# Self attentions of a four layer decoder: turns interleaved with value products, scores ahead of both, exponential ahead of the turned evictions

## What is computed

```
s = q @ k.T * scale            # 100 x 100, causal in layers 0, 1 and 3
p = softmax(s)                 # row maximum taken off, exponential, divided by the sum
y = p @ v                      # v has 8 columns a head, in layer 2 it has 16
x = x + (y @ Wo + b)           # layers 0, 1, 3
# layer 2, differential attention, two score matrices a head:
y = p1 @ v - lam * (p2 @ v);  y = y / sqrt(mean(y*y) + eps) * w;  x = x + y @ Wo
```

## Time and profile before

| | |
|---|---|
| median of three executions | 6178.4 us (6163.06 to 6204.71) |
| the profiled execution | 6208.25 us, span of the core 6206.5 us |
| PE busy | 4731.2 us, 76% of the span |
| DVE, ACT, POOL busy | 3437.1, 2441.8, 1999.7 us |
| mean granted TensorE clock | 0.818 |
| sa0, half batches (first turn to last value product) | 167.6 us |
| sa1 | 139.2 us |
| sa2 | 355.6 us |
| sa3 | 167.3 us |

### The profile page before, as it was taken

One profiled execution on the slowest core, in us unless ns is written; L12 is line 12 of the kernel. 1 busy time (PEld: TensorE's weight loads), 2 busy tenths in 40 slices (PEclk: granted clock), 3 DMA queues, 4 the chain that ended last, 5 costly groups with the idle time before them and its releaser, 6 DMA issues. The chain is left out here.

```text
span 6206.5 us, 84643 instructions
## 1 busy us (share of the span) xinstructions
PE 4731.2 (76%) x22582; PEld 3354.9 (54%) x22582; DVE 3437.1 (55%) x5067; ACT 2441.8 (39%) x3674; POOL 1999.7 (32%) x1091
## 2 busy tenths in 40 slices
PE   7999999999798866669878888888486444432698
PEld 6778778888544755348845555555274222221344
DVE  3444444444345422444556666664646999987444
ACT  2345555555222311123335555554123555540122
POOL 0055555555100000000036666664001555550000
PEclk7789999999799965687779999998677666655699
DMA  2100000000011312121111112110020000000011
GB/s 74 48 8 16 16 16 16 16 16 8 13 42 29 70 36 58 41 82 31 28 43 43 42 42 46 43 38 20 11 43 20 22 21 21 21 16 0 5 46 38
DMA packets 153375, 193.27 MB, mean 31 GB/s; under 512 B 91760, under 2 KB 136576, under 8 KB 152864
## 3 DMA queue, kind: packets, MB, share of 16 engines
q1 hardware_dynamic: 152992, 188.87, 12.5%
HBM read 134.07 MB, written 19.05 MB: 25 GB/s over the span
## 5 line engine op out<-in xcount | busy, mean ns | idle before, releaser
L1021 POOL TENSOR_TENSOR pexp_lo<-arena,pexp_hi 128x800 fp32r<-128x800 f32 x384 | 727.8, 1895 | 413.8 <-POOLq L1020 413.8
L976 POOL TENSOR_TENSOR pexp_lo<-arena,pexp_hi 128x800 fp32r<-128x800 f32 x384 | 628.4, 1636 | 515.6 <-POOLq L975 515.6
L1947 DVE TENSOR_REDUCE arena<-ps 128x1 f32<-128x482 f32 (+3 forms) x624 | 393.3, 657 | 404.1 <-DVEq L1925 388.9
L2092 DVE TENSOR_REDUCE arena<-ps 100x1 f32<-100x482 f32 (+1 forms) x768 | 476.6, 656 | 219.0 <-DVEq L2061 200.7
L1282 ACT ACTIVATE arena<-ps 128x800 f32<-128x800 f32 x384 | 322.3, 839 | 554.1 <-ACTq L1280 552.2
L1348 ACT ACTIVATE arena<-ps 128x800 f32<-128x800 f32 x384 | 321.7, 838 | 402.2 <-ACTq L1342 396.8
L2399 DVE MATCH_REPLACE8 arena<-arena 100x1444 f32<-100x1444 f32 x256 | 423.0, 1673 | 0.0
L3022 PE MATMUL ps<-kst,qs 96*100 96x482 f32 (+1 forms) x768 | 334.0, 436 | 116.4 <-PEq L2982 112.5
L1732 DVE TENSOR_REDUCE arena<-ps 100x8 f32<-100x800 f32 x160 | 158.7, 992 | 392.1 <-DVEq L1729 392.1
L3260 PE MATMUL ps<-arena,chunk 128*128 128x400 f32 x648 | 286.3, 524 | 72.6 <-PEq L3259 72.5
L2652 PE MATMUL ps<-w_const,arena 100*100 100x100 f32 x2560 | 311.2, 287 | 37.9 <-PEq L2648 37.9
(11 more groups left out here) (358 smaller groups left out, 11004.8 us busy)
## 6 DMA issues: line engine op xcount, KB each, us to landing
ctxT<-in_ctxT SPq DMA_DIRECT2D x64, 541.5 KB
ctxk<-in_ctx SPq DMA_DIRECT2D x48, 528.0 KB
kst<-mid SPq DMA_DIRECT2D x128, 180.5 KB, 3.1
heads_dram<-arena SPq DMA_DIRECT2D x20, 800.0 KB
chunk<-in_ff_chunks SPq DMA_DIRECT2D x77, 193.0 KB, 2.4
arena<-gate_dram SPq DMA_DIRECT2D x64, 200.0 KB, 3.1
kst<-xn SPq DMA_DIRECT2D x64, 180.5 KB, 2.9
q_rows<-heads_dram SPq DMA_DIRECT2D x36, 200.0 KB
```

What stands on the lines that cost most here:

```text
L976: own(nc.gpsimd.tensor_tensor(pexp_lo[p % 3][:, :, :], pexp[p % 3], pexp_hi[p % 3][:, :, :], ALU.subtract))
L1021: own(nc.gpsimd.tensor_tensor(pexp2_lo[p % 3][:, :, :], pexp2[p % 3], pexp2_hi[p % 3][:, :, :], ALU.subtract))
L1947: peak = nc.vector.tensor_reduce(mparts[0:at.stop - at.start, m, c:c + 1], bank(k, z - a, at.stop - at.start), AX.X, ALU.max)
L2092: peak = nc.vector.tensor_reduce(mparts2[:, h, c:c + 1], bank(k, z - a, S), AX.X, ALU.max)
```

## The change

PE: in each k it now waits for the exponential of k first; then come the four unread matmuls, into the score banks that scores(k + 2) will fill, then scores(k + 2), and then turns(k, k - 1): one turn of k, one value product of k - 1, and so on, eight times. The wait for o_free and v_ready (values_wait) stands ahead of the first turn, and the wait for an eviction of k - 1 ahead of each group of four. Sides follow as before. ACT: the exponential of k + 1 goes ahead of the sides and of the evictions of k. For sa2, the sums of squares (squared_sums) stay at k = 2 and the rest of finish moves to k = 3, features go to k = 4 and 5 and project to k = 6. No matmul, eviction or DMA is added or taken away.

```diff
--- before.py
+++ after.py
@@ -598,7 +598,8 @@
 
 
     VALUES_AT = {1: (0, 1, 2, 6), 2: (0, 1)}
-    TURNS_AT = {1: (3,), 2: (3, 4)}
+    TURNS_AT = {1: (3,), 2: (4, 5)}
+    PROJECT_AT = {1: 5, 2: 6}
 
     def all_units(nsm, unit):
 
@@ -1181,13 +1182,17 @@
                 if not first and k in TURNS_AT[nsm]:
                     features(k - TURNS_AT[nsm][0])
 
+            def exponential(k):
+                act.wait_ge(s.shifted, 1)
+                act.sem_inc(s.shifted, -1)
+                nc.scalar.activation(probs[:, k % 2, :].rearrange("p (c t) -> p c t", c=2),
+                                     ps[0:S, 2 * (k % 2):2 * (k % 2) + 2, 0:GT], ACT.Exp,
+                                     scale=float(cfg["scale"])).then_inc(s.probs_ready, 1)
+
             def unit(u, par, first=False, last=False):
                 for k in range(8):
-                    act.wait_ge(s.shifted, 1)
-                    act.sem_inc(s.shifted, -1)
-                    nc.scalar.activation(probs[:, k % 2, :].rearrange("p (c t) -> p c t", c=2),
-                                         ps[0:S, 2 * (k % 2):2 * (k % 2) + 2, 0:GT], ACT.Exp,
-                                         scale=float(cfg["scale"])).then_inc(s.probs_ready, 1)
+                    if k < 7 or not last:
+                        exponential((k + 1) % 8)
                     if not first and k == 2 and cfg.get("diff"):
                         root()
                     if k > 0:
@@ -1202,6 +1207,7 @@
 
             for i in range(4 // nsm):
                 value_rows(0, i, i)
+            exponential(0)
             all_units(nsm, unit)
             if cfg.get("diff"):
                 root()
@@ -1750,13 +1756,16 @@
                     dve.sem_inc(s.o_free, 1)
                     done(nc.vector.scalar_tensor_tensor(y, second, col[0:S, 6:7], y, ALU.mult, ALU.add))
 
-            def finish(par):
+            def squared_sums(par):
                 if cfg.get("diff"):
                     y = y_tok[:, par, :]
-                    y3 = y.rearrange("p (h w) -> p h w", w=16)
                     done(nc.vector.tensor_tensor(y_sq, y, y, ALU.mult))
                     done(nc.vector.tensor_reduce(y_rms[:, :], y_sq.rearrange("p (h w) -> p h w", w=16), AX.X, ALU.add))
                     dve.sem_inc(s.rms_sum, 1)
+
+            def finish(par):
+                if cfg.get("diff"):
+                    y3 = y_tok[:, par, :].rearrange("p (h w) -> p h w", w=16)
                     dve.wait_ge(s.rms_root, 1)
                     dve.sem_inc(s.rms_root, -1)
                     done(nc.vector.reciprocal(y_rms[:, :], y_rms[:, :]))
@@ -1786,6 +1795,8 @@
                     if not first and k in (0, 2):
                         normalise(k // 2 + 2, 1 - par)
                     if not first and k == 2:
+                        squared_sums(1 - par)
+                    if not first and k == nsm + 1:
                         finish(1 - par)
                     if not first and k == 7:
                         update(u - 1)
@@ -1795,6 +1806,7 @@
             all_units(nsm, unit)
             normalise(2, 1)
             normalise(3, 1)
+            squared_sums(1)
             finish(1)
             update(4 * nsm - 1)
             dve.wait_ge(s.q_stack_free, 1)
@@ -2634,41 +2646,40 @@
                     last = mm(bank(2 * (k % 2) + c, GT, S), q[:, sm, g, at], keys[:, sm, g, :, at], start=not cfg["causal"], stop=True)
                 last.then_inc(s.scores, 1)
 
-            def unread(n):
-
-                for i in range(n):
-                    mm(bank(4 + i % 2, GT, S), ident_bf[0:S, 0:S], causal_bf[:, :], start=True, stop=True)
-
-            def turn(k, first):
-                if not first:
-                    pe.wait_ge(s.probsT_ready, 2)
-                    pe.sem_inc(s.probsT_ready, -2)
-                unread(4)
-                pe.wait_ge(s.probs_ready, 1)
-                pe.sem_inc(s.probs_ready, -1)
-                for c in range(2):
-                    for j in range(4):
-                        at = c * GT + j * S
-                        last = mm(bank(4 + c, S, S, j * S), probs[:, k % 2, at:at + S], ident[0:S, 0:S], start=True, stop=True)
-                    last.then_inc(s.turned, 1)
-
-            def values(k, par):
+            def values_wait(k):
+
                 slot, half = k // 2, k % 2
-                i, sm = slot // nsm, slot % nsm
                 if half == 0:
                     pe.wait_ge(s.o_free, 1)
                     pe.sem_inc(s.o_free, -1)
-                if half == 0 and sm == 0:
+                if half == 0 and slot % nsm == 0:
                     pe.wait_ge(s.v_ready, 1)
                     pe.sem_inc(s.v_ready, -1)
+
+            def value(k, par, c, j):
+                slot, half = k // 2, k % 2
+                h = 8 * half + 4 * c + j
+                at = 16 * (vw + 1) * (slot // nsm) + h * (vw + 1)
+                ins = mm(bank(7, vw + 1, S, h * (vw + 1)), probsT[:, k % 2, c * GT + j * S:c * GT + j * S + S],
+                         vaug[:, par, at:at + vw + 1], start=True, stop=True)
+                if h == 15:
+                    ins.then_inc(s.o_full, 1)
+
+            def turns(k, behind, par):
+
+                if behind is not None:
+                    values_wait(behind)
                 for c in range(2):
+                    if behind is not None:
+                        pe.wait_ge(s.probsT_ready, 1)
+                        pe.sem_inc(s.probsT_ready, -1)
                     for j in range(4):
-                        h = 8 * half + 4 * c + j
-                        at = 16 * (vw + 1) * i + h * (vw + 1)
-                        last = mm(bank(7, vw + 1, S, h * (vw + 1)), probsT[:, k % 2, c * GT + j * S:c * GT + j * S + S],
-                                  vaug[:, par, at:at + vw + 1], start=True, stop=True)
-                if half == 1:
-                    last.then_inc(s.o_full, 1)
+                        at = c * GT + j * S
+                        ins = mm(bank(4 + c, S, S, j * S), probs[:, k % 2, at:at + S], ident[0:S, 0:S], start=True, stop=True)
+                        if j == 3:
+                            ins.then_inc(s.turned, 1)
+                        if behind is not None:
+                            value(behind, par, c, j)
 
             def features(par, c):
                 if c == 0:
@@ -2693,20 +2704,23 @@
 
             def unit(u, par, first=False, last=False):
                 for k in range(8):
-                    turn(k, first and k == 0)
+                    pe.wait_ge(s.probs_ready, 1)
+                    pe.sem_inc(s.probs_ready, -1)
+                    for i in range(4):
+                        mm(bank(2 * (k % 2) + i % 2, GT, S), ident_bf[0:S, 0:S], causal_bf[:, :], start=True, stop=True)
                     if k < 6:
                         scores(k + 2, par)
                     elif not last:
                         scores(k - 6, 1 - par)
                     if k > 0:
-                        values(k - 1, par)
-                    elif not first:
-                        values(7, 1 - par)
+                        turns(k, k - 1, par)
+                    else:
+                        turns(0, None if first else 7, 1 - par)
                     if k in VALUES_AT[nsm] and not last:
                         value_rows(u + 1, VALUES_AT[nsm].index(k))
                     if not first and k in TURNS_AT[nsm]:
                         features(1 - par, k - TURNS_AT[nsm][0])
-                    if not first and k == 5:
+                    if not first and k == PROJECT_AT[nsm]:
                         project()
 
             for i in range(per):
@@ -2716,7 +2730,10 @@
             all_units(nsm, unit)
             pe.wait_ge(s.probsT_ready, 2)
             pe.sem_inc(s.probsT_ready, -2)
-            values(7, 1)
+            values_wait(7)
+            for c in range(2):
+                for j in range(4):
+                    value(7, 1, c, j)
             for c in range(nsm):
                 features(1, c)
             project()
```

## The result

The changed kernel takes 6362.51 us (median of four executions, 6321.25 to 6405.49), the kernel before 6174.53 us on the same chip (6163.06 to 6204.71): a ratio (of the means) of 1.0297 with a 95% interval of 1.0207 to 1.0387. It is slower by 3%, 188 us. The forecast was 6300 us, slower, in a range of 6130 to 6410.

What follows compares the result with a forecast made beforehand. PE's work and its clock were taken to bound the kernel. sa2 +94, sa0 and sa3 +15 each, starts +5 made +129 us: 6337 profiled, 6307 against the median, said as 6300; range 6130 to 6410.

Steps and rivals of the forecast that it cites:

- The stall of sa2 is moved: sa2, k = 3: PE waits for o_free before its first turn, 4.9 us, against 4.3 before.
- every second unit: sa2, units 1 to 7: the clock rises in every second unit, so 59 us is taken between 55 and 63.
- the walk: sa2: a unit followed at full clock through PE, DVE and ACT; PE stands from 13.6 to 18.5 us at k = 3.
- The clock: sa2: runs free of value products shrink from 4.75 to 2.1 us, 3.6 with the projection; far fewer rises expected.
- the sum: Whole kernel: sa2 +94, sa0 and sa3 +15 each, sa1 0, starts +5; together +129 us.
- the unit: sa2, units 1 to 7: 59 us each, against some 45.6 before; 7 times 13.4 is +94 us.
- sa0 and sa3: Both stages: ten of 32 half batches at the low clock, 3.8 us dearer each; 182 us, +15 each.
- a fall lasts half a unit or more: New order: a low stretch lasts half a unit or more, in place of one or two half batches.
- The reading of sa1 against sa0: sa0 and sa3 take 167.6 and 167.3 us, sa1 139.2, for nearly the same work: difference is bias products and clock.
- The interleaved pair: Turn and value alternating on PE: taken as 0 extra; upper end 0.3 us a half batch, 48 us in 160.
- Starts: Four starts: unread matmuls now come behind the first exponential, 1.3 us each, 5 us.
- The rule that the prediction cited: Continuous work brings the clock back whatever its kind; by it the faster rival, 6103 us, would come out, chance 0.16.

Runs made afterwards that it cites:

- update late: Changed kernel with sa2's update of x put behind the normalise at k = 0 of the next unit; median 6286.92 us, ratio 1.0195 to before.
- groups of eight, four and one: Changed kernel with turns and value products in groups of eight (6233.84 us) or four (6269.06 us); one by one is the changed kernel itself (6362.51 us).
- eight unread matmuls: Changed kernel with eight unread matmuls in each half batch, not four; median 6306.31 us, ratio 1.0210 to before.
- waits off and one by one: 6060 us kernel (groups of eight, sa2's waits off the path) with alternation and the o_free wait ahead of the turns again; 6218.19 us.

## Why the prediction was right, and where it was off

- **The stall of sa2 is moved.** Right in place and size where it can occur: 4.08 us once in the changed kernel, and 3.8 to 5.5 us four times with the update late, against 4.9 worked out. But the forecast took every second unit to start at full clock and meet it. Only one did, since the wait at k = 7 stands ahead of it.
- **A wait that the walk missed.** Update, behind the projection at k = 6, holds up shift(0) and normalise(2), for 2.6 us a unit. The prediction followed what the move of finish does, and not what the move of the projection does to DVE behind it. The waits are 17 us by themselves; without them sa2 is 47 us shorter.
- **The clock.** The step that carried the sum: no run without value products, so fewer returns. The groups of eight, four and one show it, and so do the eight unread matmuls, which lengthen the run and leave the alternation. Three of the four returns in sa2 came where the prediction put them, at the projection, the fourth behind a row product; with the waits off and one by one every return after the first unit was at a projection. sa2 was forecast at +94 us and measured +132. The term that was too small is the unit: 59 us in the sum, a mean of 64 in the trace (units 1 to 7 from 2797.45 on), more than the 63 of a unit low throughout, since the waits at k = 7 added 2.4 us a unit and three of four returns were lost there after 3 to 4 us. The first unit fell as well, behind a wait of 0.50 us, where I had let only stalls of several microseconds count. The low stretches of before, 13.5 to 27.5 us each, were two to four half batches, not the one or two that the prediction names.
- **sa0 and sa3.** Forecast +15 each, measured +26 and -13. sa0 had a low stretch of 92 us with PE busy throughout; sa3 had six short ones, 18 us together. That a fall lasts half a unit or more was wrong for sa3: four of its falls came at a bias product, as at 4714.04, and the clock was back after 3 to 3.5 us. Here bias and row products, unread matmuls, masks and scores make a run of 3.5 us without a value product (4714.04 to 4717.54), where sa2 has 2.1. The same run didn't help sa0 for 92 us, and what decides it the runs don't show. Two of the experiments with the same code for sa0 have it at 155. The +15 was right for neither stage.
- **The bias products.** The reading of sa1 against sa0 held: without them the clock is at 0.99.
- **The interleaved pair.** Taken as free, with at most 0.3 us a half batch. Measured at full clock 0.35 us a pair (2779.97 to 2780.32), 2.8 us for eight, against 2.70 apart; but unread matmuls and scores take as much less, and a half batch is 3.83 us from unread matmul to unread matmul (2774.41 to 2778.24), against 3.84. Free it was.
- **Starts.** 1.3 us each were expected: too small to be told apart here.
- **The median** lies 62 us above the forecast of 6300, within its range. In the profiled execution, 41 us under the median, the four stages are 150 us longer, where the sum had 129: sa2 38 more than forecast, sa1 5 more, sa0 and sa3 together 17 less, the starts not told apart. That part of sa2's excess was offset by sa0 and sa3 is luck. The rest can't be assigned; the four executions of the changed kernel differ by 84 us.

The rule that the prediction cited, the Trainium skill's "TensorE: Matmul & The Clock Gate", Part 1, is that activity releases the throttle and idle time brings it back. The runs agree that the clock falls behind idle time, at waits of 0.8 us five times of five, at 0.5 us sometimes; they also have falls with no idle time, at the bias products (in sa0 of the changed kernel, at 130 us of its span). They don't agree that continuous work is enough to bring the full clock back: with the update late 155.00 busy microseconds of 155 stayed at 0.50.

What stays open: whether the low clock in mixed runs comes from the few columns that a value product streams, or from something else in which it differs from a turn. No run here changes the columns alone. Open is also why the same short wait is followed by a fall in one execution and not in another.

## What to carry to other kernels

A PE that is always busy isn't a PE at full speed: cut the stage out, read its granted clock, and look at which kinds of matmul stand around each fall and each return. Where short products can't be avoided, keep the dense matmuls together, so that the clock has somewhere to return, and take small waits off the path before anything is made even; an even mixture holds the full clock only as long as nothing waits and nothing else disturbs it (sa1: 136 us at the full clock, until the wait near its end). When a side job is moved to a later step, walk the queue of every engine that waits for it, not only the one that the move was meant for.

## What the runs showed of the hardware

- A low clock can hold under steady work: 71 us in sa2 of the changed kernel, 92 us in its sa0 and 155 us in sa2 with the update late, PE busy throughout.
- A wait of 0.50 us stood ahead of such a stretch (2779.97), and the same wait at the same place in three other kernels (2735.21 with the update late, and in groups of eight and of four) had no fall behind it. Waits of 4.3 to 4.9 us before the change were each followed by 13.5 to 27.5 us of low clock.
- Four more unread matmuls a half batch, 110 us of added work, didn't make the changed kernel slower (6306 against 6362 us).
- Bias products of one row, 12 a stage at 0.4 us, cost 28 us a stage, 5 of them their own time and 23 through the clock.
